# Causal attention and feed-forward block on one core: row maxima copied into the score banks by ScalarE, three score passes instead of four, and the first chunk's output projection moved into the last head pair

## The chip, the cores and the metric

One core of one Trainium2 chip runs the whole program. The metric is the device time of one execution in microseconds (us), lower is better. TensorE (PE) does matmuls, VectorE (DVE) and ScalarE (ACT) elementwise work, GpSimd (POOL) elementwise work that does not touch the matmul results, SyncE (SP) issues the DMAs.

## What is computed

From the reference, cut to what matters (two sequences of 2048 rows, model width 256, 16 heads of width 64, hidden width 768, all in fp32):

```python
hn = layernorm(h) * gamma + beta
q, k, v = rope(hn @ Wq + bq), rope(hn @ Wk + bk), hn @ Wv + bv
attn = softmax(where(tril, q @ k.T / 8, -inf)) @ v
x = layernorm(h + (attn @ Wo + bo + h))
gate, up = x @ wg, x @ wu                      # weights are int32 / 127
out = layernorm(x + (silu(gate) * up) @ wd)
```

## The kernel before

**Two stages.** The first does the attention, head pair by head pair: 8 pairs for each of 2 sequences, 16 iterations, called FIRST, MIDDLE, SWITCH (where the sequence changes) and LAST. The second is the output projection and the feed-forward, in 8 chunks of 512 rows. Matrix operands are held as a high part (`fp32r`) and a remainder, and a product is three matmuls: high by high, remainder by high, high by remainder (`product`, L1017 to L1020).

**One pair.** The scores are computed transposed, keys on partitions, in 40 units of 128 keys by up to 512 queries (`UNITS`: block of 512 queries, key tile). 28 units have all 512 queries; on the diagonal there are also four each of 384, 256 and 128. Two units make a group, 20 groups `g` make a pair. For each unit, both heads go through the array side by side (two halves of 64 rows, banks `s_ps[two]` and `s_ps[two + 1]`): three passes for the product (L1084, L1086, L1088) and a fourth (L1090) that adds minus the row's maximum, a matmul of a constant `ones_r` with `aux`. `aux` holds the negated maxima of 512 queries as rows. Diagonal units add a mask (L1094). Then ScalarE takes the exponent of both banks into `pt` (L517), TensorE multiplies by the values (`weigh`, L1115, one group later), and GpSimd adds `pt` up for the softmax sum (L458). `pt` has 5 slots, and the score banks hold two units.

**Maxima.** They are found ahead of the scores, by matmuls in the other orientation (`maxima`, L1063, bank pair `m_ps`) and a max reduction on VectorE (L731) into `mc`; the next matmul into `m_ps` waits for the reduction (`maxed`). In each group, one goes before the scores and one behind them; `AHEAD` is how many units they are ahead. For a block of 512 queries VectorE then spreads the eight columns of `mc` into the zeroed `mz` (`spread`, L745), TensorE transposes `mz` (L1101) and ScalarE copies the result to `aux` (L501).

**Work for the next pair.** Within a pair the next pair's projections are made through one shared bank `x_ps`. The table `XUSE` says which group uses that bank for what: Q0 to Q3 and K0 to K3 are the pieces of the query and key projection, V0 to V3 the values, M the transpose of maxima, R the softmax sums (`sums`, L1122). A Q or K piece goes: six matmuls; ScalarE adds the bias (`piece_raw`, L490); four DMAs swap halves; VectorE multiplies by the cosine (L764), one group later by the sine (L770) and adds (L774); another group later ScalarE rounds (`piece_hi`, L495) and VectorE forms the remainder (`piece_lo`, L779).

**Queues.** Every engine has its own in-order queue, written out by hand in the function `pair` of that engine. On ScalarE a group is: eviction of an output block, `piece_hi`, two exponents, `weights`, `shifts` (the copy to `aux`), `piece_raw`. On VectorE: spread, turn of the sums, cosine, values, the reductions, sine and add, division of an output block, `piece_lo`.

**Second stage.** For each chunk: `load_o` brings the attention output back from memory, `attn_hi` on ScalarE (L525) and `attn_lo` on VectorE (L803) split it into `o_t`, `project_out` multiplies by `Wo` (96 matmuls into `y_ps`), `add_residual` and `first_norm` make `x1_g`, `turn_x1` transposes it, `ffn_up` is 72 matmuls into `gu_ps`, `hidden` is the work of ScalarE and VectorE on them, `ffn_down` is 72 matmuls into `z_ps`, `second_norm` ends the chunk. `cycle(c)` on TensorE is `ffn_up(c)`, `turn_x1(c + 1)`, `project_out(c + 2)`, `ffn_down(c)`. The splits of chunk c + 2 are done one in each step of `hidden(c)`, the last ones behind it.

## Time and profile before

| | |
|---|---|
| median of 3 runs | 2352.92 us (2342.64 to 2354.73) |
| profiled execution | 2344.87 us, its span 2343.1 us |
| mean granted TensorE clock | 0.964 |
| busy, share of the span | PE 92%, PE weight loads 60%, DVE 72%, ACT 41%, POOL 61% |
| attention stage | to about 1970 us of the span |
| output projection and feed-forward | from there to 2343 us |
| one MIDDLE pair | about 116 us |
| DMA | 100.45 MB, mean 43 GB/s |

Matmuls are pipelined, so a matmul's duration is longer than the time until the next one may start; starts of successive rows tell the pace. The two heads' matmuls of one pass run side by side and stand in one row as x2.

### The profile page before, as it was taken

The page shows a single profiled execution, that of the slowest core. Times are in us where ns is not written, and L with a number is a line of the kernel's source. Part 1 is how long each engine was busy: PE and PEld are TensorE (multiplying, and loading weights), DVE is VectorE, ACT ScalarE, POOL GpSimd, SP SyncE. Part 2 cuts the span into 40 slices and gives each one's busy share as a digit, 9 for nine tenths or more (in the row PEclk, how much of TensorE's full clock was granted, in tenths as well). Part 3 has the DMA queues.
Part 4 walks back from the last instruction along what each step waited for, and adds up shares of the span by engine and source line. Part 5 has one row for each costly group of instructions (what it writes and reads, how often), then busy time and mean ns, then how long its engine had stood idle before and what let it go on. Part 6 is the DMA issues. An engine that isn't in the chain of part 4 may idle for free.

```text
span 2343.1 us, 43529 instructions
## 1 busy us (share of the span) xinstructions
PE 2155.6 (92%) x15872; PEld 1415.6 (60%) x15872; DVE 1685.4 (72%) x2313; ACT 957.0 (41%) x1300; POOL 1433.4 (61%) x1204
## 2 busy tenths in 40 slices
PE   5689999999999999899999999999999996898997
PEld 4446565556555655555656565656565654787886
DVE  8567878787878787778787878787878762556544
ACT  3333444344444443334444444343434443334332
POOL 2447777777777777577878787777777785000000
PEclk8799999999999999899999999999999998899998
DMA  5100111011101112101010101010101031212200
GB/s 162 62 19 24 40 31 34 28 38 30 34 27 39 32 33 67 28 24 40 24 40 24 40 24 41 24 41 24 40 24 41 23 109 54 90 64 70 91 9 28
DMA packets 79468, 100.45 MB, mean 43 GB/s; under 512 B 13968, under 2 KB 43664, under 8 KB 78992
## 3 DMA queue, kind: packets, MB, share of 16 engines
q1 hardware_dynamic: 79248, 97.60, 14.0%
q8 instruction: 128, 2.10, 0.4%
q14 instruction: 92, 0.75, 0.1%
HBM read 40.93 MB, written 23.07 MB: 27 GB/s over the span
## 4 chain that ended last, share of the span: by engine, by line
PE 74%; DVE 17%; issue 5%; ACT 1%; DMA 1%; SPq 1%; POOL 0%; DVEq 0%; POOLq 0%; ACTq 0%
PE o_ps L1115 17%; PE m_ps L1063 8%; DVE mpart L731 6%; PE x_ps L1018 6%; PE s_ps L1084 5%; PE x_ps L1020 4%; PE x_ps L1019 4%; PE s_ps L1086 4%; PE s_ps L1090 4%; PE s_ps L1088 4%; PE gu_ps L1018 2%; PE gu_ps L1020 2%; PE gu_ps L1019 2%; PE y_ps L1018 2%; PE x_ps L1122 2%
## 5 line engine op out<-in xcount | busy, mean ns | idle before, releaser
L458 POOL TENSOR_TENSOR acc<-acc,pt 128x512 f32<-128x512 f32 (+3 forms) x1024 | 1233.8, 1236 | 227.0 <-ACT pt L517 226.3
L731 DVE TENSOR_REDUCE mpart<-m_ps 128x2 f32<-128x1024 f32 (+2 forms) x576 | 625.7, 1086 | 346.7 <-PE m_ps L1063 209.7
L517 ACT ACTIVATE pt<-s_ps 128x1024 f32<-128x1024 f32 (+3 forms) x640 | 545.1, 896 | 568.3 <-PE s_ps L1090 319.0
L1115 PE MATMUL o_ps<-pt,v 128*64 128x512 f32 (+3 forms) x2560 | 558.5, 558 | 1.5 <-ACT pt L517 1.5
L1063 PE MATMUL m_ps<-qk 64*128 64x512 f32 (+3 forms) x1280 | 286.1, 442 | 97.2 <-DVE mpart L731 79.4
L1063 PEld LDWEIGHTS m_ps<-qk 64*128 64x128 f32 x1280 | 122.0, 186 | 378.0 <-issue 217.0
L1115 PEld LDWEIGHTS o_ps<-pt,v 128*64 128x64 f32 x2560 | 159.3, 139 | 236.7 <-issue 213.6
L453 POOL TENSOR_TENSOR acc<-pt 128x512 f32<-128x512 f32 (+1 forms) x128 | 165.1, 1310 | 204.1 <-ACT pt L517 204.1
L1084 PE MATMUL s_ps<-qk 64*128 64x512 f32 (+3 forms) x1280 | 249.2, 384 | 0.0
L1086 PE MATMUL s_ps<-qk 64*128 64x512 f32 (+3 forms) x1280 | 235.6, 363 | 0.0
L1090 PE MATMUL s_ps<-aux,ones_r 64*128 64x512 f32 (+3 forms) x1280 | 235.6, 362 | 0.0
L1088 PE MATMUL s_ps<-qk 64*128 64x512 f32 (+3 forms) x1280 | 234.9, 361 | 0.0
L495 ACT ACTIVATE qk<-qc 128x512 fp32r<-128x512 f32 x128 | 80.4, 631 | 289.3 <-DVE qc L774 289.3
L774 DVE TENSOR_TENSOR qc<-qc,rot 128x512 f32<-128x512 f32 x128 | 174.3, 1362 | 4.4
L1018 PE MATMUL x_ps<-w_hl,hn 128*128 128x128 f32 x496 | 140.6, 284 | 0.0
L1020 PE MATMUL x_ps<-w_hl,hn 128*128 128x128 f32 x496 | 137.7, 278 | 0.0
L1019 PE MATMUL x_ps<-w_hl,hn 128*128 128x128 f32 x496 | 137.6, 278 | 0.0
L490 ACT ACTIVATE qr<-x_ps,b_qk 128x512 f32<-128x512 f32 x120 | 82.4, 687 | 132.3 <-PE x_ps L1020 132.3
L770 DVE TENSOR_TENSOR rot<-rot,sin_sb 128x512 f32<-128x512 f32 x128 | 128.1, 1001 | 8.0 <-DMA rot<-qr 8.0
L1086 PEld LDWEIGHTS s_ps<-qk 64*128 64x128 f32 x1280 | 122.4, 186 | 18.7
L1088 PEld LDWEIGHTS s_ps<-qk 64*128 64x128 f32 x1280 | 122.0, 185 | 19.3
L1090 PEld LDWEIGHTS s_ps<-aux,ones_r 64*128 64x128 f32 x1280 | 122.1, 186 | 19.1
(151 smaller groups left out, 3426.0 us busy)
## 6 DMA issues: line engine op xcount, KB each, us to landing
rot<-qr SPq DMA_DIRECT2D x512, 64.0 KB, 2.0
attn<-o_n SPq DMA_DIRECT2D x64, 256.0 KB, 2.1
o_raw<-attn SPq DMA_DIRECT2D x8, 2048.0 KB, 8.9
w_raw<-in_wqkv SPq DMA_DIRECT2D x51, 128.0 KB, 2.6
h_g<-in_h SPq DMA_DIRECT2D x8, 512.0 KB, 3.5
out<-out_g SPq DMA_DIRECT2D x8, 512.0 KB, 3.2
qk_place<-in_h SPq DMA_DIRECT2D x4, 512.0 KB, 5.5
pt<-in_h SPq DMA_DIRECT2D x4, 512.0 KB, 11.0
```

What stands on the lines that cost most here:

```text
L458: nc.gpsimd.tensor_tensor(sums, sums, probs, ALU.add).then_inc(summed, 1)
L517: nc.scalar.activation(pt[:, u % SLOTS, :, q0:NB], s_ps[:, two:two + 2, q0:NB], ACT.Exp, scale=SCALE)\
L731: nc.vector.tensor_reduce(dst, m_ps[:, :, 0:w], AX.X, ALU.max, negate=True).then_inc(maxed, 1)
L1018: nc.tensor.matmul(dst, lhs[0], rhs[0], start=first, stop=False)
L1019: nc.tensor.matmul(dst, lhs[1], rhs[0], start=False, stop=False)
L1020: return nc.tensor.matmul(dst, lhs[0], rhs[1], start=False, stop=last)
L1063: last = nc.tensor.matmul(m_ps[:, a, 0:w], qk[par][rows, 0, q], qk[par][rows, 1, k], start=True, stop=not diag)
L1084: nc.tensor.matmul(dst[a], qk[par][rows, 1, k], qk[par][rows, 0, q], start=True, stop=False)
L1086: nc.tensor.matmul(dst[a], qk[par][rows, 1, k], qk[par][rows, 2, q], start=False, stop=False)
L1088: nc.tensor.matmul(dst[a], qk[par][rows, 3, k], qk[par][rows, 0, q], start=False, stop=False)
L1090: last = nc.tensor.matmul(dst[a], ones_r[rows, :], aux[rows, q0:NB], start=False, stop=not diag)
L1115: last = nc.tensor.matmul(o_ps[rows, q0:NB], v[par][:, j, rows], pt[:, u % SLOTS, a, q0:NB], start=(j == 0), stop=(j == n - 1), skip_group ...
```

## The change

- **Score banks.** The fourth score pass is taken out, with `ones_r` and `aux`. In its place ScalarE copies the negated maxima (`shift`, both heads, 512 queries) from SBUF into the unit's two score banks before the scores (`shift_unit`, one copy of up to 128x1024 for each unit, behind the two exponents of the group before), and the three matmul passes all add onto what the bank holds (`start=False`). The scores wait for that copy (`shifted`) instead of for the exponent (`exped`). Before the first pair two identity matmuls write the two banks of the second unit once (`banks_whole`), and two copies are made ahead.
- **Transposes of maxima.** `spread` and `mz` are gone. `turn_maxima` runs once for each head: four matmuls with a column of `mc`, repeated over 128 columns, as the weights, and `id_r`, the identity as `fp32r`, as the data, so that all 128 partitions get the row. ScalarE evicts each of the two into `shift`. The second head's turn follows behind `weigh` of the same group, and waits for ScalarE's eviction of the first.
- **Order.** `AHEAD` is 20 instead of 18; `XUSE` is rearranged; VectorE does cosine and values before it turns the sums.
- **Start.** VectorE makes `id_r` before its first statistics, so it waits for `ln_in`, the third of three small loads that follow the input on the DMA queue.
- **Last pair.** The feed-forward weights are split in groups 5, 7, 9, 11 instead of 9, 11, 13, 15. In groups 12 to 19 the first chunk's attention output is split into buffers of its own (`o_first`), and its projection runs before the last `weigh` and the last `sums`; its residual and norm run before the last division.
- **Second stage.** Chunk 0's `ffn_up` comes before chunk 1's projection. The splits of the chunk ahead start `EARLY = 4` steps before `hidden` and so end earlier. The last chunk's final norm and store are done in two halves.

The core of the diff (buffers, semaphores and wait values left out):

```diff
-AHEAD = 18
+AHEAD = 20
-XUSE = {0: "R3", 1: "M1", 2: "R0", 3: "Q0", 4: "K0", 5: "M2", 6: "R1", 7: "Q1", 8: "K1", 9: "V0", 10: "Q2", 11: "M3",
-        12: "R2", 13: "K2", 14: "V1", 15: "Q3", 16: "V2", 17: "K3", 18: "V3", 19: "M0"}
+XUSE = {3: "Q0", 4: "M20", 5: "K0", 6: "V0", 7: "Q1", 8: "K1", 9: "Q2", 10: "M30", 11: "K2", 12: "V1", 13: "Q3",
+        14: "V2", 15: "K3", 16: "V3", 17: "M01", 19: "M11"}
+SUMMED = {0: 3, 2: 0, 6: 1, 12: 2}
-FFN_SPLIT = {9: 0, 11: 1, 13: 2, 15: 3}
+FFN_SPLIT = {5: 0, 7: 1, 9: 2, 11: 3}
+OUT_SPLIT = {g: range(g - 12, g - 11) for g in range(12, 20)}
...
+            def shift_unit(n, u, first=False):
+                blk, j, q0 = UNITS[u]
+                two = 2 * (u % 2)
+                if not first:
+                    act.wait_ge(exped, n * NU + (u - 1))
+                if j <= 1:
+                    act.wait_ge(shift_in, n * (2 * BLOCKS) + 2 * (blk + 1))
+                nc.scalar.activation(s_ps[:, two:two + 2, q0:NB], shift[:, blk % 2, :, q0:NB], ACT.Copy)\
+                  .then_inc(shifted, 1)
...
                     for u in group_units(g):
                         exp_unit(kind, it, u)
+                    for u in group_units(g + 1):
+                        if not first_shift and (u < NU or kind is not LAST):
+                            shift_unit(it + u // NU, u % NU)
...
+            dve.wait_ge(ln_in, 16 * 3)
+            nc.vector.tensor_copy(id_r[:, :], id_f[:, :]).then_inc(id_rounded, 1)
             input_group(0)
...
             def scores(kind, it, par, u):
-                if kind is not FIRST or u >= 2:
-                    pe.wait_ge(exped, it * NU + (u - 1))
+                pe.wait_ge(shifted, it * NU + (u + 1))
...
                 for a, rows in enumerate(halves):
-                    nc.tensor.matmul(dst[a], qk[par][rows, 1, k], qk[par][rows, 0, q], start=True, stop=False)
+                    nc.tensor.matmul(dst[a], qk[par][rows, 1, k], qk[par][rows, 0, q], start=False, stop=False,
+                                     skip_group_check=True)
...
-                for a, rows in enumerate(halves):
-                    last = nc.tensor.matmul(dst[a], ones_r[rows, :], aux[rows, q0:NB], start=False, stop=not diag)
...
-            def turn_maxima(n, blk):
-                pe.wait_ge(mz_done, n * BLOCKS + (blk + 1))
+            def turn_maxima(n, blk, a):
...
                 for t in range(TG):
-                    last = nc.tensor.transpose(x_ps[:, t * P:(t + 1) * P], mz[:, t, :], id_f[:, :])
+                    last = nc.tensor.matmul(x_ps[:, t * P:(t + 1) * P], mc[:, blk, t, a:a + 1].broadcast_to([P, P]),
+                                            id_r[:, :], start=True, stop=True)
...
             def hidden(c, ahead):
+                if ahead is not None:
+                    for k in range(EARLY):
+                        attn_hi(ahead, k)
...
-            pe.wait_ge(cw_lo, 4)
             pe.wait_ge(maxed, 2 * PAIRS * NM)
             pe.wait_ge(c_lo, OC)
-            project_out(0)
+            project_out(0, o_first)
+            weigh(LAST, FINAL, 1, NG - 1)
+            pe.wait_ge(r_turned, FINAL * BLOCKS + 3)
+            sums(FINAL, BLOCKS - 1)
+            turn_x1(0)
+            ffn_up(0, True)
             pe.wait_ge(c_lo, 2 * OC)
             pe.wait_ge(x_added, 1)
             project_out(1)
-            turn_x1(0)
-            ffn_up(0, True)
+            ffn_down(0)
+            next_turn(0)
             next_out(0)
-            next_turn(0)
-            ffn_down(0)
```

## Rows read from the trace of the kernel before

**Rows 1.** Stretches, one MIDDLE and the LAST: PE, PEld, DVE, ACT, POOL; clock; DMA.

```profile
1256.00:1372.00 116.00, 112.89 (x866) 68.63 (x866) 91.09 (x110) 49.99 (x65) 88.90 (x75) 0.99 0.12 32
...
1838.00:1970.00 132.00, 118.10 (x894) 65.50 (x890) 69.07 (x79) 57.48 (x69) 110.17 (x96) 0.95 0.16 55
```

**Rows 2.** Timeline of VectorE, one group with pieces in work (in brackets: idle before).

```profile
1454.66 0.74 DVE L764 SCALAR_TENSOR_TENSOR qc<-x_ps,b_qk,cos_sb 128x512 f32<-128x512 f32 x1
1455.32 1.21 DVE L731 TENSOR_REDUCE mpart<-m_ps 128x2 f32<-128x1024 f32 x1
1457.18 1.23 DVE L731 TENSOR_REDUCE mpart<-m_ps 128x2 f32<-128x1024 f32 x1 [0.65 <-PE m_ps L1063]
...
1459.08 1.65 DVE L774 TENSOR_TENSOR qc<-qc,rot 128x512 f32<-128x512 f32 x1
1460.65 1.76 DVE L779 TENSOR_TENSOR qk<-qc,qk 128x512 fp32r<-128x512 f32 x1
```

**Rows 3.** Timeline at the end of the last pair.

```profile
1932.90 34.46 POOL L458 TENSOR_TENSOR acc<-acc,pt 128x512 f32<-128x512 f32 x28 [0.25 <-ACT pt L517]
...
1967.50 1.97 PE L1122 MATMUL x_ps<-acc,ones_f 128*64 128x512 f32 x4 [8.14 <-POOL acc L458]
1976.95 0.55 PE L1018 MATMUL y_ps<-wo_hl,o_t 128*128 128x256 f32 x1 [7.47 <-DVE o_t L803]
```

**Rows 4.** Waits from 2050 us on (total us, times, longest).

```profile
PE y_ps L1018 <- DVE o_t L803: 18.1, 5, 3.6
```

**Rows 5.** Timeline of TensorE, end of one unit (start, duration).

```profile
1456.29 0.39 PE L1088 MATMUL s_ps<-qk 64*128 64x512 f32 x2
1456.52 0.40 PE L1090 MATMUL s_ps<-aux,ones_r 64*128 64x512 f32 x2
```

**Rows 6.** Timeline of TensorE, the transposes of maxima and what follows.

```profile
1402.60 0.66 PE L1101 MATMUL x_ps<-id_f,mz 128*128 128x128 f32 x4
1403.18 1.72 PE L1115 MATMUL o_ps<-pt,v 128*64 128x512 f32 x8
```

**Rows 7.** Groups by line and shape (count, busy us, mean ns, idle before).

```profile
L517 ACT ACTIVATE pt<-s_ps 128x1024 f32<-128x1024 f32 x448 | 440.3, 1025 | 482.5 <-PE s_ps L1090 319.0 <-PE s_ps L1094 161.4 <-POOL acc L458 2.0
...
L745 DVE COPY mz<-mc 128x8 f32<-128x8 f32 x64 | 51.0, 797 | 0.1
...
L627 ACT ACTIVATE x_keep<-x_g 128x1024 f32<-128x1024 f32 x8 | 8.5, 1058 | 14.8 <-DVE out_g L979 14.8
```

**Rows 8.** Timeline of ScalarE in the same groups.

```profile
1452.80 0.69 ACT L490 ACTIVATE qr<-x_ps,b_qk 128x512 f32<-128x512 f32 x1 [0.81 <-PE x_ps L1020]
1454.77 0.63 ACT L495 ACTIVATE qk<-qc 128x512 fp32r<-128x512 f32 x1 [1.29 <-DVE qc L774]
1456.04 1.95 ACT L517 ACTIVATE pt<-s_ps 128x1024 f32<-128x1024 f32 x2 [0.63 <-PE s_ps L1090]
```

**Rows 9.** Timeline at the start of the span: DVE's statistics, PE's first transpose.

```profile
4.48 1.40 DVE L690 BATCH_NORM_STATS2 stats<-qk_place 128x6 f32<-128x256 f32 x4 [2.78 <-DMA qk_place<-in_h]
...
10.22 1.11 PE L1032 MATMUL s_ps<-id_f,qk_place 128*128 128x128 f32 x4 [10.22 <-DMA bet<-in_beta]
```

**Rows 10.** Groups by line: add in the pairs, remainder in the second stage.

```profile
L774 DVE TENSOR_TENSOR qc<-qc,rot 128x512 f32<-128x512 f32 x128 | 174.3, 1362 | 4.4
...
L803 DVE TENSOR_TENSOR o_t<-o_raw,o_t 128x512 fp32r<-128x512 f32 x64 | 42.1, 683 | 0.0
```

**Rows 11.** Busy time by stretch: first projection, first ffn_up, first ffn_down.

```profile
1976.90:1990.40 13.50, 13.33 (x96) 13.15 (x96) 0.01 (x1) 0.03 (x1) 0.00 (x0) 0.87 0.45 158
...
2012.60:2029.00 16.40, 16.32 (x72) 13.44 (x72) 9.93 (x16) 9.10 (x16) 0.00 (x0) 1.00 0.10 32
...
2048.70:2057.30 8.60, 8.60 (x73) 8.56 (x72) 7.25 (x19) 2.92 (x5) 0.00 (x0) 1.00 0.21 64
```

**Rows 12.** Timeline at the end of the span: VectorE's last chunk, SyncE's store.

```profile
2334.35 1.23 DVE L979 SCALAR_TENSOR_TENSOR out_g<-z_ps,x_keep 128x1024 f32<-128x1024 f32 x1 [6.48 <-PE z_ps L1020]
...
2339.65 0.37 SPq L323 DMA_DIRECT2D out<-out_g  x1
```

More of the change, by code:

```diff
@@ L82, in sem @@
             return ctx.enter_context(nc.semaphore(name))
+        with nc.sbuf_tensor("o_first_hi", [P, OC * NB], F32R) as o_first_hi:
+            pass
         cos_sb = sb("cos_sb", [P, SEQ], F32)
@@ L152, in postln_block_kernel @@
         wo_hl = split_sb("wo_hl", OC * DM)
+        with nc.sbuf_tensor("o_first_lo", [P, OC * NB], F32R) as o_first_lo:
+            pass
+        o_first = [o_first_hi[:, :], o_first_lo[:, :]]
         wg_raw = sb("wg_raw", [P, KC * HID], I32)[:, :]
@@ L555, in pair @@
                         split_ffn(FFN_SPLIT[g])
+                    if g in OUT_SPLIT and kind is LAST:
+                        for k in OUT_SPLIT[g]:
+                            act.wait_ge(cw_lo, 4)
+                            attn_hi(0, k, o_first)
             def affine(i):
@@ L609, in _ @@
             rounded(3)
-            shifts(0, 0)
+            for a in range(2):
+                shifts(0, 0, a)
             for i in range(TURNS):
                 next_affine(i)
+            act.wait_ge(cos_done, 8)
+            act.wait_ge(banks_whole, 1)
+            for u in range(2):
+                shift_unit(0, u, True)
             each_pair(act, pair)
@@ L840, in pair @@
                         split_ffn(FFN_SPLIT[g])
+                    if g in OUT_SPLIT and kind is LAST:
+                        for k in OUT_SPLIT[g]:
+                            attn_lo(0, k, o_first)
             def rest(i):
@@ L898, in _ @@
             for m in range(TG):
[L899 removed]
+                maximum(0, m, False)
             turned(2)
             remainders(1)
[L902 removed]
             unturned(3)
@@ L955, in hidden @@
             def hidden(c, ahead):
+                if ahead is not None:
+                    for k in range(EARLY):
+                        attn_lo(ahead, k)
                 for m in range(MC + 1):
@@ L968, in hidden @@
                           .then_inc(hid_lo, 1)
-                    if ahead and m < MC:
-                        attn_lo(c + 2, m)
-                if ahead:
-                    for k in range(MC, OC):
-                        attn_lo(c + 2, k)
+                    if ahead is not None and EARLY + m < OC:
+                        attn_lo(ahead, EARLY + m)
             def second_norm(c, par, n):
@@ L983, in second_norm, with last_norm, cycle @@
                 nc.vector.memset(pause[:, :], 0.0).then_inc(tile_done, 1)
-            def cycle(c, par, ahead):
+            def last_norm(half):
+                c, before = CHUNKS - 1, (2 * CHUNKS - 1) * (2 * TG + 1)
+                tiles = range(HALF_TILES * half, HALF_TILES * (half + 1))
+                here = slice(tiles[0] * DM, (tiles[-1] + 1) * DM)
+                dve.wait_ge(z_done, c + 1 + half)
+                if half == 0:
+                    dve.wait_ge(x_kept, c + 1)
+                    dve.wait_ge(out_stored, c * 16 + 16)
+                nc.vector.scalar_tensor_tensor(out_g[:, here], z_ps[:, here], DEQ, x1_keep[c % 2][:, here],
+                                               ALU.mult, ALU.add).then_inc(z_added, 1)
+                dve.wait_ge(z_added, c + 2 + half)
+                norm(out_g, 2 * CHUNKS - 1 + half, out_rows, before + half * (2 * HALF_TILES + 1), tiles)
+                dve.wait_ge(out_rows, c * TG + HALF_TILES * (half + 1))
+                nc.vector.memset(pause[:, :], 0.0).then_inc(tile_done, 1)
+            def cycle(c, par, ahead=None):
                 hidden(c, ahead)
@@ L988, in cycle @@
                 second_norm(c - 1, 1 - par, c * 2 + 1)
-                if ahead:
+                if ahead is not None:
                     add_residual(c + 2)
                     first_norm(c + 2, c * 2 + 2)
-            for k in range(OC):
-                attn_lo(0, k)
-            add_residual(0, True)
-            for k in range(OC):
-                attn_lo(1, k)
-            first_norm(0, 0)
-            x1_lo(0)
-            add_residual(1)
-            hidden(0, True)
-            first_norm(1, 1)
+            add_residual(0, True)
+            first_norm(0, 0)
+            turn_sums(FINAL, BLOCKS - 1)
+            invert(FINAL, BLOCKS - 1)
+            divide(FINAL, BLOCKS - 1)
+            x1_lo(0)
+            hidden(0, 1)
+            add_residual(1)
+            first_norm(1, 1)
+            for k in range(OC):
+                attn_lo(2, k)
             x1_lo(1)
@@ L1216, in _, with project_out @@
             pe.wait_ge(v_done, 4)
+            for i in range(2, 4):
+                last = nc.tensor.matmul(s_ps[:, i, :], id_r[:, :], hn[:, 0, 0, 0:NB], start=True, stop=True)
+            last.then_inc(banks_whole, 1)
             each_pair(pe, pair)
-            weigh(LAST, FINAL, 1, NG - 1)
-            pe.wait_ge(r_turned, FINAL * BLOCKS + 3)
-            sums(FINAL, BLOCKS - 1)
-            def project_out(c):
+            def project_out(c, src=o_t):
                 for t in range(TG):
```

274 lines of the change are left out of this document (144 added, 130 removed).

## The prediction

> **What bounds the kernel now.** I read the busy time by stretch first, then the timelines of one middle pair engine by engine, then the waits. A middle pair takes about 116 us, and TensorE is busy for 112.9 of them at a clock of 0.99; VectorE is busy for 91.1, GpSimd for 88.9, ScalarE for 50.0 [rows 1]. The reader is to see that TensorE sets the pace but that two engines stand only a fifth behind it, so a saving on TensorE can't be taken in full. In each group TensorE can't pass its second maxima until VectorE has reduced the first; with pieces in work VectorE needs from 1454.66 to 1462.41, 7.75 us, for one group, its wait for the second maxima included [rows 2]. The last pair is another stage: it takes 132 us, GpSimd is busy for 110.2 [rows 1] and works without a pause over the last 34.5 us [rows 3]. The second stage is TensorE again, with gaps in which it waits for the split of the attention output [rows 3, 4].
>
> **The score passes.** One pass over 512 queries costs TensorE 0.23 us, 1456.29 to 1456.52; the two heads run side by side [rows 5]. The durations in the row, 0.39, overlap and would give twice as much. The 40 units of a pair have 28 x 512 + 4 x (384 + 256 + 128) = 17,408 of 20,480 queries, 0.85, so a pair saves 40 x 0.23 x 0.85 = 7.8 us.
>
> **The transposes.** Four of them now take 0.58 us (1402.60 to 1403.18) [rows 6]; four times that is 2.3 us a pair. Eight sets replace them. I take 0.5 us each, 4.0 us: they are no wider than those. Bounds are 0.3 and 0.66. That gives back 1.7 us. A second turn also waits for ScalarE to evict the first. Where the next group is narrow (M20, M30) the eviction comes in time, since `weigh` covers it. For M01 ScalarE stands behind two exponents and two copies until about 5.2 us after the group's first score, and TensorE is there at 4.1: 1.1 us. For M11 I count 0.4. Together 1.5 us. So TensorE's own path is 7.8 - 1.7 - 1.5 = 4.6 us shorter.
>
> **The copies on ScalarE.** No copy from SBUF into a score bank is in this trace. The nearest rows are the exponent of 1024 columns, 1025 ns and 0.98 us from one to the next, and the SBUF copy of 1024, 1058 ns [rows 7, 8]. I take the exponent's pace, 34 us a pair; bounds are 0.7 and 1.5 us for a full unit. With four more evictions ScalarE goes from 50 to about 87 us of a pair, so it isn't full. Its place in the chain matters more. A group of 512s with a Q or K piece would take TensorE 6 x 0.23 for the scores, 0.66 for maxima, 1.6 for the piece and 1.9 for `weigh`: 5.5 us. In it ScalarE starts exponents 0.9 us in, ends them at 2.9, ends the two copies at 4.8, and only then evicts the piece (`piece_raw`, 0.69 [rows 8]), at 5.5 instead of 4.5. The next group's first scores can start at 3.9 as far as the copy goes. This is covered, with 1.6 us to spare; groups without a piece (3.9 us) have nothing to spare and stall 0.1 to 0.3 us, eight of them a pair. Queued behind a late `piece_raw` are the swap DMAs and the cosine, and behind the cosine the reductions.
>
> **VectorE.** It loses the spread, 0.8 us x 4 = 3.2 us a pair [rows 7], and gets the second maxima 0.23 to 0.46 us earlier. In the stretch of groups 7 to 10, whose pieces are on VectorE at the same time, it still needs 6 to 7.5 us a group where TensorE would need 5.5. I take 1.5 us a pair more waiting for maxima than now and 1.5 us for the small stalls and the late cosine, and against them the 3 us by which spreads no longer delay the reductions: nothing net. This is a choice between the bounds, not a reading. A middle pair then saves 4.6 us. Bounds: 0 (VectorE and ScalarE keep the pace that TensorE gives up) and 7.0 (the wait for the spread was in the way too and no new stall appears). 14 such pairs: 64 us.
>
> **Start and first pair.** VectorE now waits for the small loads, which are in at 10.2 us, where its statistics began at 4.48 [rows 9]. Of the 5.7 us, 2.2 are absorbed where it later waits for a weight split; 3.6 us remain. Two turns and evictions ahead of the first pair, two copies before its first scores and one before its third group: 1.2 + 1.9 + 1.9. Its own saving is small, since the first maxima bind it: 3.6 us. Net loss 5 us; bounds 0 and 9.
>
> **Last pair.** GpSimd sets it, so three passes save nothing behind group 6. Eight remainders move in beside it. The add on VectorE takes 1362 ns beside a busy GpSimd, and the same form takes 683 ns where GpSimd is idle [rows 10]: the two get in each other's way. The weight splits leave groups 12 to 15 for it. I take 0; bounds are 4 us less and 8 x 0.68 = 5.5 us more.
>
> That speaks against the change, and the Trainium skill has the rule (SBUF — State Buffer, Who interferes with whom): a VectorE instruction with two SBUF inputs and a GpSimd one that reads SBUF exclude each other for the whole instruction. By this rule each remainder put into the last pair would lengthen the engine that sets its end, and the sum would be 5.5 us higher than mine. The row agrees that there is interference and doesn't show who pays.
>
> **Second stage, first chunks.** Now TensorE idles 8.1 and 7.5 us around the last sums [rows 3], and the first projection takes 13.5 us at a clock of 0.87; the reader may compare 72 matmuls of `ffn_down` at 1.00 in 8.6, which is 11.5 us for 96 [rows 11]. With the change the projection runs while GpSimd finishes, ends at about 1973 in the old time, and residual, norm (6 us), a last division on VectorE (2.4) and the transposes bring `ffn_up(0)` to about 1983. Then 18 us for it (a cold start), 11.5 + 8.6 for projection 1 and `ffn_down(0)`, 1 + 1.4 for transposes and a wait, 11.5 for projection 2: 2035, where `ffn_up(1)` began at 2057.3. That saves 22 us; bounds 14 and 27.
>
> **Five later chunks.** Each now waits 3.6 us for the split, 18.1 in all [rows 4], after which its projection runs for 13.3 us instead of 11.5. With four splits ahead, all eight are done by the fourth step of `hidden`, some 8 us before TensorE asks. 5 x (3.6 + 1.8) = 27 us less; I take 26, bounds 12 and 29. Next late would be the x1 split, which has the whole projection as cover.
>
> **The end.** From TensorE's last result to the store issue are 5.3 us [rows 12]; of the second half about 3.3 remain, and its store is half as large: 2.5 us less.
>
> **Sum.** 5 - 64 + 0 - 22 - 26 - 2.5 = -109.5. The profiled execution took 2344.9 us for a span of 2343.1; the median is 2352.9, 8 us above it, and I take the difference off the median: 2243.4, say 2244.
>
> **Rivals.** (1) The whole pass comes through: 7 us a pair, 34 more than forecast, 2210. For it: TensorE waits for VectorE only a few us a pair; against it: VectorE's busy groups [rows 2], which a faster TensorE runs into. (2) The pairs give nothing, because VectorE and the longer chain through ScalarE hold the old pace: 14 x 4.6 back, 2308. For it speaks that VectorE's group of 7.75 us is longer than TensorE's of 5.5 [rows 2]; against it, that such groups are few and the spread leaves it. (3) On the other side: ScalarE becomes the bound. If a copy into the score banks costs 1.5 us, a full group with a piece has 1.95 + 3.0 + 0.69 + 0.63 = 6.3 us of ScalarE against 5.5, and with the fixed order each of some 14 full groups grows by 0.7 or more: 9 us a pair over the forecast, 14 x 9 = 126 more, 2370. It decides from about 1.4 us a copy, where the pairs lose as much as the second stage gives. For it: ScalarE doubles its load in the loop; against it: both nearest rows are at 1.05.
>
> **Chances.** Forecast (pairs save 2.5 to 6 us each) 0.57, its own range 2218 to 2276; rival 1 0.12; rival 2 0.23; rival 3 0.08. Leaving out rival 3 and the far edges of 1 and 2, the range is 2203 to 2314. A change within 0.5%, 12 us, is about what a measurement of this kernel can't tell from none. Faster: the first three cases but the worst tenth of rival 2, 0.89. The rest of that and the mild part of rival 3 make 0.04 for the same. Slower: 0.07.
>
> **What would show it.** The profile of the changed kernel should show three rows of L-numbers under `s_ps` with starts 0.23 apart, 640 copies of `shift` near 1.0 us, a middle pair of about 111.5 us with ScalarE at 87, VectorE at 88, `y_ps` without a wait in the later chunks, the first projection before the last `x_ps` sums, and VectorE's first statistics after 10 us. Wrong would make it: copies much over 1 us, waits of the scores for `shifted`, waits of `m_ps` for the reductions above 10 us a pair, or a last pair that GpSimd ends later by more than 5 us.

## The result and the profile after

The changed kernel takes 2482.5 us, median of 4 runs (2471.2 to 2488.0), against 2353.8 for the kernel before in the same set. The ratio is 1.0551, 95% interval 1.0504 to 1.0597: 129 us slower. The forecast was 2244. The profiled execution has a span of 2477.1 us at a mean granted clock of 0.940, where the span before was 2343.1 at 0.964.

The loss has one place. Milestones are the first score of the second pair, the first score of the last pair, the first matmul of `ffn_up(1)`, and the end:

| stretch | before, us | after, us | difference | forecast |
|---|---|---|---|---|
| start and first pair | 222.2 | 241.8 | +19.6 | +5 |
| 14 pairs | 1648.1 | 1799.9 | +151.8 | -64 |
| last pair to `ffn_up(1)` | 186.7 | 173.0 | -13.7 | -22 |
| `ffn_up(1)` to the end | 286.1 | 262.4 | -23.7 | -28.5 |
| span | 2343.1 | 2477.1 | +134.0 | -109.5 |

So the last two stretches gave 37 of the 50.5 us forecast, and the 14 pairs missed by 216 us. Within those pairs the loss sits in groups 6 to 14, where most of the pieces stand: they took 53.2 us of a pair before and take 66.1 now, the other eleven groups 64.5 and 62.5 (means of the 14 pairs, from one group's first score to the next's). The busy time of those 14 pairs, of the kernel before:

```profile
222.20:1870.30 1648.10, 1584.13 (x12100) 967.41 (x12098) 1287.06 (x1534) 702.76 (x918) 1241.85 (x1036) 0.98 0.12 33
```

and of the changed one, with one quiet pair of it below (columns as in [rows 1], whose first row it answers to):

```profile
241.80:2041.70 1799.90, 1602.31 (x11204) 935.51 (x11204) 1326.43 (x1478) 1164.78 (x1535) 1227.12 (x1036) 0.95 0.11 30
...
1406.83:1530.84 124.01, 108.97 (x806) 64.14 (x806) 94.38 (x105) 83.19 (x110) 87.86 (x74) 0.99 0.11 31
```

TensorE's idle time went from 64.0 to 197.6 us. That is 133.6 of the 151.8. The rest is busy time, which grew by 18 although a pass is gone. Part of that is the clock: a mean of 0.95 between the two levels of 1.2 and 2.4 GHz means a tenth of the stretch at the lower one, 180 us, where 0.98 meant 66. At most half of that difference, 57 us, is lost by it (an estimate; the rounding of the two means leaves 40 to 74). ScalarE, at 83 of 124 us, is not full.

The copies cost what was forecast, 1035 ns for a full one beside an exponent of 1023 (groups by shape, changed kernel; compare [rows 7]):

```profile
L531 ACT ACTIVATE s_ps<-shift 128x1024 f32<-128x1024 f32 x448 | 446.4, 1035 | 1.0 <-issue 0.9
L548 ACT ACTIVATE pt<-s_ps 128x1024 f32<-128x1024 f32 x448 | 438.1, 1023 | 383.1 <-PE s_ps L1141 312.5 <-PE s_ps L1146 68.4 <-POOL acc L478 2.1
```

What TensorE waits for (total, times, longest) in those 14 pairs, before:

```profile
PE m_ps L1063 <- DVE mpart L731: 56.4, 59, 4.0
PE m_ps L1063 <- issue: 5.9, 4, 1.8
```

and changed:

```profile
PE m_ps L1115 <- DVE mpart L780: 101.8, 90, 6.0
PE m_ps L1115 <- DVE mc L780: 33.7, 20, 2.2
PE x_ps L1180 <- DVE v L792: 27.1, 25, 1.6
PE m_ps L1115 <- issue: 11.7, 4, 3.4
PE x_ps L1158 <- ACT shift L521: 11.4, 14, 0.9
```

VectorE's share grew from 56.4 to 162.6 us, 106 of the 133.6. The same list over the whole run, before:

```profile
PE m_ps L1063 <- DVE mpart L731: 79.4, 81, 4.0
```

and changed:

```profile
PE m_ps L1115 <- DVE mpart L780: 133.1, 117, 6.0
PE m_ps L1115 <- DVE mc L780: 37.6, 25, 2.2
PE x_ps L1180 <- DVE v L792: 27.6, 27, 1.6
PE x_ps L1158 <- ACT shift L521: 18.3, 17, 5.1
PE m_ps L1115 <- issue: 11.7, 4, 3.4
```

Three of the five name VectorE. Its operations with two SBUF inputs also became longer: the add and the remainder (L774 and L779 before) and the division (L798 before) took 1362 [rows 10], 1004 and 772 ns and now, in the groups by line, take (mean ns behind the comma)

```profile
L812 DVE TENSOR_TENSOR qc<-qc,rot 128x512 f32<-128x512 f32 x128 | 193.6, 1512 | 4.4
L817 DVE TENSOR_TENSOR qk<-qc,qk 128x512 fp32r<-128x512 f32 x128 | 168.9, 1322 | 0.0
L836 DVE TENSOR_TENSOR o_n<-o_sum,r_b 128x512 f32<-128x512 f32 x64 | 65.0, 1016 | 7.0 <-DVE r_b L830 0.3
```

With the sine product (L770 before, 128.1 us; L808 now, 138.5) these four lines took 480 us of VectorE before and take 566, 86 more, where the spreads that went had taken 51 [rows 7].

The wait for `v` was not in the forecast at all. Here it is in the timeline of the quiet pair, group 6, in which a values piece and block 1's sums now share the bank:

```profile
1440.52 1.66 DVE L808 TENSOR_TENSOR rot<-rot,sin_sb 128x512 f32<-128x512 f32 x1
...
1442.10 0.87 PE L1173 MATMUL o_ps<-pt,v 128*64 128x256 f32 x8
1442.21 1.65 DVE L812 TENSOR_TENSOR qc<-qc,rot 128x512 f32<-128x512 f32 x1
...
1443.78 0.68 DVE L792 TENSOR_TENSOR v<-x_ps,b_v 128x512 f32<-128x512 f32 x1
...
1444.59 1.08 PE L1180 MATMUL x_ps<-acc,ones_f 128*64 128x512 f32 x4 [1.62 <-DVE v L792]
1445.60 0.50 PE L1115 MATMUL m_ps<-qk 64*128 64x512 f32 x2
1445.71 0.72 DVE L822 STREAM_TRANSPOSE r_t<-x_ps 128x512 f32<-128x512 f32 x1 [1.25 <-PE x_ps L1180]
...
1446.35 1.19 DVE L780 TENSOR_REDUCE mpart<-m_ps 128x2 f32<-128x1024 f32 x1
```

The last piece matmul started at 1441.89, so the values could have been taken out at about 1442.2. VectorE, in its fixed order, did the sine product and the addition first, and the sums waited 1.62 us. Then VectorE stood 1.25 us for those sums, with the next reduction queued behind. In group 10 the reduction stands behind four other jobs:

```profile
1462.48 1.54 DVE L808 TENSOR_TENSOR rot<-rot,sin_sb 128x512 f32<-128x512 f32 x1
...
1464.05 1.65 DVE L812 TENSOR_TENSOR qc<-qc,rot 128x512 f32<-128x512 f32 x1
...
1465.62 1.76 DVE L817 TENSOR_TENSOR qk<-qc,qk 128x512 fp32r<-128x512 f32 x1
...
1467.31 0.74 DVE L802 SCALAR_TENSOR_TENSOR qc<-x_ps,b_qk,cos_sb 128x512 f32<-128x512 f32 x1
...
1467.97 0.41 DVE L780 TENSOR_REDUCE mc<-m_ps 128x2 fp32r<-128x256 f32 x1
...
1468.43 0.39 PE L1115 MATMUL m_ps<-qk 64*128 64x256 f32 x2 [2.02 <-DVE mc L780]
```

The maxima were ready at about 1464.9; the reduction took 0.41 us and began 3.1 us later.

### The profile page after: what moved, and what is told of

It reads as the page before. It is cut to its first block, busy times and chain, and to the rows that moved or that the text cites. A ratio compares the mean times of both kernels' runs of the same rounds, so it can differ in the third digit from the quotient of the medians.

```text
span 2477.1 us, 42394 instructions
## 1 busy us (share of the span) xinstructions
PE 2169.4 (88%) x14850; PEld 1368.9 (55%) x14850; DVE 1730.0 (70%) x2255; ACT 1486.7 (60%) x2005; POOL 1420.2 (57%) x1204
## 4 chain that ended last, share of the span: by engine, by line
PE 46%; DVE 23%; issue 15%; ACT 6%; DMA 2%; POOL 2%; SPq 2%; DVEq 0%; ACTq 0%; POOLq 0%
PE o_ps L1173 10%; DVE mpart L780 10%; PE m_ps L1115 7%; PE x_ps L1180 3%; DVE rot L808 3%; PE x_ps L1070 2%; ACT pt L548 2%; DMA rot<-qr 2%; ACT s_ps L531 2%; POOL acc L478 2%; PE x_ps L1072 2%; PE x_ps L1071 2%; PE s_ps L1135 2%; SPq L348 2%; PE x_ps L1158 2%
## 5 line engine op out<-in xcount | busy, mean ns | idle before, releaser
L478 POOL TENSOR_TENSOR acc<-acc,pt 128x512 f32<-128x512 f32 (+3 forms) x1024 | 1216.6, 1223 | 387.7 <-ACT pt L548 387.1
L780 DVE TENSOR_REDUCE mpart<-m_ps 128x2 f32<-128x1024 f32 (+2 forms) x576 | 625.8, 1086 | 390.3 <-PE m_ps L1115 236.3
L1173 PE MATMUL o_ps<-pt,v 128*64 128x512 f32 (+3 forms) x2560 | 579.1, 576 | 0.0
L531 ACT ACTIVATE s_ps<-shift 128x1024 f32<-128x1024 f32 (+3 forms) x640 | 551.1, 906 | 1.0 <-issue 0.9
L1115 PE MATMUL m_ps<-qk 64*128 64x512 f32 (+3 forms) x1280 | 306.1, 474 | 196.2 <-DVE mpart L780 133.1
L1135 PE MATMUL s_ps<-qk 64*128 64x512 f32 (+3 forms) x1280 | 254.8, 394 | 4.4 <-ACT s_ps L531 4.4
L1141 PE MATMUL s_ps<-qk 64*128 64x512 f32 (+3 forms) x1280 | 238.5, 367 | 0.0
L1138 PE MATMUL s_ps<-qk 64*128 64x512 f32 (+3 forms) x1280 | 238.5, 368 | 0.0
L812 DVE TENSOR_TENSOR qc<-qc,rot 128x512 f32<-128x512 f32 x128 | 193.6, 1512 | 4.4
L817 DVE TENSOR_TENSOR qk<-qc,qk 128x512 fp32r<-128x512 f32 x128 | 168.9, 1322 | 0.0
L521 ACT ACTIVATE shift<-x_ps 128x512 f32<-128x512 f32 x128 | 76.6, 598 | 117.3 <-PE x_ps L1158 117.3
L808 DVE TENSOR_TENSOR rot<-rot,sin_sb 128x512 f32<-128x512 f32 x128 | 138.5, 1082 | 8.0 <-DMA rot<-qr 6.3
L1070 PE MATMUL x_ps<-w_hl,hn 128*128 128x128 f32 x496 | 142.7, 288 | 0.0
L1072 PE MATMUL x_ps<-w_hl,hn 128*128 128x128 f32 x496 | 140.6, 283 | 0.0
L1071 PE MATMUL x_ps<-w_hl,hn 128*128 128x128 f32 x496 | 139.9, 282 | 0.0
L1135 PEld LDWEIGHTS s_ps<-qk 64*128 64x128 f32 x1280 | 126.2, 193 | 24.5 <-ACT s_ps L531 15.7
L1138 PEld LDWEIGHTS s_ps<-qk 64*128 64x128 f32 x1280 | 125.3, 192 | 19.8
```

Of the source, the lines that this page charges most:

```text
L478: nc.gpsimd.tensor_tensor(sums, sums, probs, ALU.add).then_inc(summed, 1)
L531: nc.scalar.activation(s_ps[:, two:two + 2, q0:NB], shift[:, blk % 2, :, q0:NB], ACT.Copy)\
L780: nc.vector.tensor_reduce(dst, m_ps[:, :, 0:w], AX.X, ALU.max, negate=True).then_inc(maxed, 1)
L808: nc.vector.tensor_tensor(rot[:, a, :], rot[:, a, :], sin_sb[:, NB * c:NB * (c + 1)], ALU.mult)\
L812: nc.vector.tensor_tensor(qc[:, c % 2, a, :], qc[:, c % 2, a, :], rot[:, a, :], ALU.add).then_inc(roped, 1)
L1070: nc.tensor.matmul(dst, lhs[0], rhs[0], start=first, stop=False)
```

## The experiments

Each run's ratio is to the kernel before on the same chip; 1% is 23.5 us. The 95% intervals are plus or minus 0.002 to 0.005. "Against the changed kernel" is the difference of the ratios in us, so good to some 12 to 16 us. Where the text gives pairs or groups without a trace, they are times from first score to first score, as means of the 14 pairs: 117.7 us a pair before, 128.6 in the changed kernel.

| run | median us | ratio | against the changed kernel |
|---|---|---|---|
| e1 the end alone | 2312.9 | 0.9843 | |
| e13 the scores alone | 2506.6 | 1.0691 | |
| e2 sums in groups of their own | 2551.4 | 1.0852 | +71 |
| e3 no copies | 2447.1 | 1.0405 | -34 |
| e5 fourth pass again | 2481.3 | 1.0557 | +1 |
| e7 second maxima late | 2554.9 | 1.0868 | +74 |
| e6 first reduction ahead | 2461.7 | 1.0474 | -18 |
| e9 values between | 2447.7 | 1.0423 | -30 |
| e10 both | 2422.6 | 1.0330 | -52 |
| e14 and a turn off the loop's edge | 2418.0 | 1.0308 | -57 |
| e4 / e8 halved reductions, changed / before | 2356.6 / 2268.0 | 1.0030 / 0.9651 | -122 / (-82 of before) |
| e11 / e12 halved additions, changed / before | 2362.7 / 2287.9 | 1.0080 / 0.9759 | -111 / (-57 of before) |
| e15 e10 with halved reductions | 2314.9 | 0.9884 | -157 |
| e17 with halved additions too | 2214.5 | 0.9436 | -262 |
| e18 instead without copies | 2243.8 | 0.9559 | -233 |
| e16 the end, and first reduction ahead | 2293.6 | 0.9777 | |

### Which half loses (e1, e13)

e1 is the kernel before with the change's edits from the last pair on (`FFN_SPLIT`, `OUT_SPLIT`, `o_first`, `EARLY`, the new order of chunks, the last chunk in halves); e13 is the rest of the change (`AHEAD`, `XUSE`, `shift`, `id_r`, VectorE's order, three passes).

> The kernel before with everything that the change does from the last pair on (first chunk's output split and projected in the last pair, four tiles split early, last chunk in halves), and none of what it does to the scores: four passes, the maxima's passes and copies of before. Theory A (the loss is in the attention pairs, and the second part of the change is worth what the two traces show from the last pair's start, 472.8 us before against 435.4 after): about 2315 us, between 2305 and 2325. Rival (the two parts lean on each other, the gain at the end came from a pair that was late anyway): 2340 to 2360.

> The other half of the first run: what the change does to the scores, and nothing of what it does from the last pair on. If the two halves add up (2482.5 changed, 2312.9 with the end alone, 2350 before): 2515 to 2525. If the gain at the end depends on the pairs: 2485 to 2510.

The end alone gains 37 us (0.9843, interval 0.9813 to 0.9873), as A said. The scores alone lose 162 (1.0691). Together that is 125 lost against 129 measured, within the intervals. The median of e13, 2506.6, is 8 us under the range for halves that add up and lies in the other one (2485 to 2510); but the kernel before was at 2344 in that set and not at 2350, and by the ratio the halves add up.

### Does the removed pass matter (e5)

```diff
+                for a, rows in enumerate(halves):
+                    nc.tensor.matmul(dst[a], qk[par][rows, 1, k], qk[par][rows, 2, q], start=False, stop=False, ...)
                 for a, rows in enumerate(halves):
                     last = nc.tensor.matmul(dst[a], qk[par][rows, 3, k], qk[par][rows, 0, q], ...
```

> The changed kernel with the fourth pass back in each score unit, as a second go at the second pass (it adds that term twice, so the scores are not the reference's). Everything else stays, the copies too. Theory A2 (between the two maxima units of a group TensorE now has two score units of 0.70 us, 1.40 in all, where it had 1.86, and VectorE's 1.22 us reduction with a cosine or values of 0.7 in front no longer fits beneath; the pass that was removed was cover): the pass costs next to nothing, 2470 to 2500. Rival (TensorE is the bound, the pairs are longer for another reason): the pass costs its 7 us in each of 16 pairs, 2580 to 2600.

A whole pass put back, 7.8 us of TensorE in every pair by the forecast's count, costs nothing, as A2 said; the waits for `mpart` fall from 133.1 to 99.9 us. TensorE doesn't set these pairs. But with this cover restored the time doesn't fall either, so the missing pass is not what makes them 11 us longer; that must be in what came with it.

### ScalarE's copies (e3)

```diff
-                pe.wait_ge(shifted, it * NU + (u + 1))
+                if kind is not FIRST or u >= 2:
+                    pe.wait_ge(exped, it * NU + (u - 1))
...
-                    for u in group_units(g + 1):
-                        if not first_shift and (u < NU or kind is not LAST):
-                            shift_unit(it + u // NU, u % NU)
```

> The changed kernel without ScalarE's 640 copies of the shift into the score banks: the first of the three passes starts the bank, and waits for the exponents of two units before as the kernel before does. It leaves the maxima out of the scores (they are still reduced, turned and copied to SBUF). Theory A (VectorE's order of work and the shared bank make the pairs longer): 2440 to 2480, the pairs stay over 120 us. Rival B (the copies cost it): the pairs fall to the forecast 111 us or below, 2230 to 2300 in all.

34 us come back, not 200: rival B falls as the main cause and stays as a part. By the two traces 9.6 us of it are in the first pair (163.6 and 154.0) and 24.5 in the 14 pairs, 1.75 each. Half of that is group 17: 6.09 us from its first score to the next group's, 5.17 without the copies. There the second turn of maxima waits for ScalarE's eviction, which is queued behind two exponents and two copies.

### VectorE's order (e2, e7, e6, e9, e10, e14)

```diff
-XUSE = {3: "Q0", 4: "M20", 5: "K0", 6: "V0", 7: "Q1", 8: "K1", 9: "Q2", 10: "M30", 11: "K2", 12: "V1", 13: "Q3",
-        14: "V2", 15: "K3", 16: "V3", 17: "M01", 19: "M11"}
+XUSE = {2: "V0", 3: "Q0", 4: "M20", 5: "K0", 7: "Q1", 8: "K1", 9: "Q2", 10: "M30", 11: "K2", 13: "V1", 14: "Q3",
+        15: "V2", 16: "K3", 17: "M01", 18: "V3", 19: "M11"}
```

> The changed kernel with one edit: the shared bank's table. The sums of blocks 1 and 2 (groups 6 and 12) have the bank to themselves again; only block 0's sums, in the light group 2, share it with a values piece. Theory A1 (the pairs lose to the sums that wait in TensorE for VectorE's values and to VectorE that then waits for the sums, ahead of its reductions): about 3 us a pair come back, 2430 to 2450. Rival B (the copies on ScalarE cost it, by their chain exponents - copy - scores or by what they do to the other engines): nothing, 2475 to 2490. Rival C (VectorE simply has too much in a group, wherever the sums stand): at most 1 us a pair, 2465 to 2485.

```diff
                 for i, m in enumerate(list(ms)[:len(ms) - len(held)]):    # held = the second unit, not in FIRST
...
                         project_v(it + 1, VALUES[g], 2)
+                    for m in held:
+                        pe.wait_ge(maxed, it * NM + m)
+                        maxima(it, par, m) if m < NM else maxima(it + 1, 1 - par, m - NM)
```

> The changed kernel with TensorE's order changed in all pairs but the first: a group's second maxima unit stands behind the turn or the projection piece, ahead of the weighing, so that the reduction of the first has the two score units and the piece (1.4 us and some 2 to 2.6 us) as cover, and the next group's first unit only the weighing. Theory A2: 2400 to 2450. Rival C: 2470 to 2490, or slower where the weighing alone (about 0.9 us) is too short a cover for the second reduction.

Both miss their theory's range by 100 us and more, on the slow side; e2 lies outside every range, and e7 where its rival C said "or slower". In e2 the wait for values is gone from groups 6 and 12, and the waits of `m_ps` for `mpart` rise from 133.1 to 180.9 us: emptying TensorE's groups doesn't empty VectorE's, and the pieces pile up in the neighbours (group 7 from 5.9 to 10.4 us). In e7 a later reduction pushed cosine and values back, and TensorE waited 51 us for `qc` and 63 for `v`. Moving TensorE's work about is no remedy when VectorE's queue is what is late. The next three change that queue:

```diff
+                    early = ms[:1] if ended is None and kind is not FIRST else []   # e6; e10: after sums too
+                    for m in early:
+                        reduction(m)
                     if g - 1 in PIECE and kind is not LAST:
                         cosine(it + 1, *PIECE[g - 1], 1 - par, 2)
...
                   .then_inc(rope_mul, 1)
+                if between is not None:      # e9 and e10: values(...) in groups 6 and 12
+                    between()
```

> The changed kernel with VectorE's order changed in the groups after no sums, in all pairs but the first: the group's first reduction stands ahead of the cosine or the values of the piece before, not behind. Theory A2 (the second maxima unit waits for a reduction that stands behind another job): 1 to 4 us a pair, 2420 to 2465. Rival C (VectorE's total in a group sets the pace, the order doesn't matter): 2470 to 2490.

> The changed kernel with one job of VectorE moved: in the two groups of a pair where a values piece and sums share the bank (6 and 12), it takes the values out between the sine product and the addition of the same group, not behind both at the start of the next group. Theory A1 (the sums wait about 1.8 us in TensorE for the values, twice a pair, and the clock falls behind such a gap): 2 to 4 us a pair, 2420 to 2450. Rival (the wait only moves to VectorE, which has the same work to do): 2470 to 2490.

> The run before this, and with it each group's first reduction ahead of the cosine, the values and the turn of the sums, in every group of all pairs but the first (the values no longer depend on the next group, so this can be done after sums too). Theories A1 and A2 together: the 1.8 us waits and part of the waits for reductions go, 2380 to 2430. Rival C (VectorE's total in a group paces): within 10 us of the run before this.

All three come out as A1 and A2 said. In e9 groups 6 and 12 go from 8.9 and 7.5 us to 7.2 and 7.3, and the wait for `v` leaves the list. But the 52 us of e10 are not all a loss that the change brought. The kernel before, too, has its reductions behind the cosine and the values, and there the same early reduction gives 15 us (e16 against e1), about what it gives here (18, e6). What e9 mends, the values and sums in one group, came with the change: 30 us. Better order is worth 52 us, and some 30 of the 162 are shown to be the new order's.

```diff
-        14: "V2", 15: "K3", 16: "V3", 17: "M01", 19: "M11"}
+        14: "V2", 15: "K3", 16: "V3", 17: "M01", 18: "M11"}
```

> The kernel with values between and each first reduction ahead (2422.6), and with the next pair's second turned maxima moved from group 19 to group 18, so that the last group of a pair, behind which the loop over pairs turns back, has no wait for ScalarE's copy between two turns. Theory E (at the loop's edge TensorE stood 2.7 us for issue behind the second turn, where the kernel before stood 1.3, and the clock halved behind it, so that group 19 took 5.1 and 8.0 us by turns): 2 to 3 us per pair with an edge and a little in the others, 2395 to 2412. Rival (the edge costs the same wherever the turn stands): 2418 to 2426, or more, if group 18 grows by what 19 loses.

The move is worth 5 us, less than the intervals can tell; the median lies 6 us outside theory E's range, at the lower end of its rival's. Groups 18 and 19 together take 9.2 us in most pairs. In the four pairs that end at the loop's edge they took 15.0, 15.1, 11.8 and 11.8 us, and now take 13.9, 14.5, 11.0 and 11.4. At that edge the changed kernel (timeline; the matmul of L1138 takes 0.40 at the full clock) shows what followed an idle stretch:

```profile
1530.22 0.69 PE L1115 MATMUL m_ps<-qk 64*128 64x384 f32 x2 [2.71 <-issue]
...
1531.42 0.64 PE L1138 MATMUL s_ps<-qk 64*128 64x512 f32 x2
```

with the granted clock (last but two of the columns) at 0.76 and 0.56 around it:

```profile
1526.80:1531.80 5.00, 2.29 (x16) 1.79 (x16) 0.72 (x1) 0.60 (x1) 0.61 (x2) 0.76 0.04 10
1531.80:1536.80 5.00, 5.00 (x32) 2.57 (x28) 1.62 (x3) 3.88 (x6) 2.71 (x4) 0.56 0.00 0
1536.80:1541.80 5.00, 4.36 (x44) 2.57 (x44) 4.04 (x6) 2.74 (x4) 2.24 (x4) 1.00 0.01 2
```

### VectorE's pace (e4, e8, e11, e12)

```diff
-                nc.vector.tensor_reduce(dst, m_ps[:, :, 0:w], AX.X, ALU.max, negate=True).then_inc(maxed, 1)
+                nc.vector.tensor_reduce(dst, m_ps[:, :, 0:w // 2], AX.X, ALU.max, negate=True).then_inc(maxed, 1)
```

> The changed kernel with each reduction over the first half of its bank's columns only (the maxima are those of half the keys), so that a reduction of 1.22 us becomes about 0.65, some 44 us less of VectorE's 94 a pair... the passes are untouched. Theory A and C (TensorE waits for VectorE's reductions, 12 us more a pair than before): the waits m_ps <- VectorE go and the pairs fall to 110 or less, 2200 to 2300 us. Rival B (ScalarE's copies pace the scores): 2420 or more.

> The kernel before with each reduction over the first half of its bank's columns, as the changed kernel had it in the run before this: the control. Theory A2 (with four passes the reductions are all but covered): 1 to 2 us a pair, its waits m_ps <- VectorE were 3 on PE in the pair shown, so 2315 to 2340, against the 126 us that the same edit gave the changed kernel. Rival (the reductions pace both kernels alike): 2230 or less.

Less work on VectorE gives the changed kernel 122 us. That is 57 us short of the range of A and C: the pairs come down to 120.9 us, not to 110, so something else holds them too. It gives the kernel before 82, where I expected 10 to 35 and the rival 120 or more: that kernel was held by VectorE as well. Its waits of 79.4 us for `mpart` were the sign. With the same edit in both, the changed kernel is still 89 us behind (1.0030 against 0.9651).

```diff
-                            nc.gpsimd.tensor_tensor(sums, sums, probs, ALU.add).then_inc(summed, 1)
+                            part = slice(0, (NB - q0) // 2)
+                            nc.gpsimd.tensor_tensor(sums[:, part], sums[:, part], probs[:, part], ALU.add)...
```

> The changed kernel with GpSimd's additions of the softmax sums from each block's third unit on over half of their columns (the sums of the other half lack their terms). Theory D (the loss is made larger by GpSimd: VectorE's operations with two SBUF inputs took 1512, 1322 and 1016 ns beside it where the kernel before had 1362, 1004 and 772): these fall to 1.0, 0.8 and 0.7 us, VectorE has 8 us a pair less, 2370 to 2430. Rival (A1, A2: the waits are of order, not of pace): the operations fall, the time by less than 20 us.

> The control: the same edit in the kernel before. Theory D in its strict form (the contention is what the change brought): less than a third of what the edit gives the changed kernel, 2335 to 2350. Rival (the contention slows both, the changed kernel only stands nearer to VectorE's limit): 10 to 25 us, 2325 to 2340.

e11 ends 7 us below theory D's range. e12 goes as its rival said, both kernels gain, but its size is beyond both: 57 and 111 us, the changed kernel twice as much (46 and 108 of them in the 14 pairs). With this edit in both, the changed kernel is 75 us behind. Nothing on VectorE was edited, and its operations became shorter (groups by line, e11):

```profile
L814 DVE TENSOR_TENSOR qc<-qc,rot 128x512 f32<-128x512 f32 x128 | 147.6, 1153 | 4.4
L819 DVE TENSOR_TENSOR qk<-qc,qk 128x512 fp32r<-128x512 f32 x128 | 116.2, 911 | 0.0
L838 DVE TENSOR_TENSOR o_n<-o_sum,r_b 128x512 f32<-128x512 f32 x64 | 54.5, 852 | 7.0 <-DVE r_b L832 0.3
```

The reduction, which reads PSUM, did not (1088 ns here, 1086 in the changed kernel). The Trainium skill states the same (SBUF — State Buffer, Who interferes with whom): a VectorE instruction with two SBUF inputs contends with a GpSimd one that reads SBUF, and `tensor_reduce` on trn2 doesn't. e11 agrees on both. In e12 the picture is less even: the addition fell from 1362 to 954 ns, the remainder only from 1004 to 938, and the division rose from 772 to 942.

### What is left when both are mended (e15, e17, e18)

The edits are those above: e15 has e10's and e4's, e17 also e14's and e11's, e18 instead of e11's has e3's.

> The kernel with values between and each first reduction ahead, and with every reduction over the first half of its columns (maxima of half the keys). Theory A and C together (order and pace of VectorE are all that keeps the pairs from their forecast length): pairs of 111 to 115 us, 2230 to 2270 in all. Rival (something else too, the second turns or the copies, holds the pairs): 118 to 120, as with the halved reductions alone, 2300 to 2350.

> The kernel with VectorE's new order and halved reductions (2314.9), with the second turned maxima in group 18, and with GpSimd's additions over half their columns too (sums of half the columns lack terms). If what is left above the forecast pairs is VectorE's pace beside GpSimd: its operations with two SBUF inputs come down to about 0.9 us and the pairs to 110 to 112, 2210 to 2250. If it is the copies: 2290 to 2315.

> The same kernel with GpSimd's additions whole again and without ScalarE's 640 copies (the maxima are left out of the scores). If the copies hold what is left: 2210 to 2250. If it is VectorE beside GpSimd: 2280 to 2310, and the copies are worth at most the 35 us that they were in the changed kernel.

Order and halved reductions together leave pairs of 118 us: my claim that they are all was wrong, and the rival's 2300 to 2350 holds the result. (The turn in group 18 is in e17 and e18 too; it is worth 5 us.) GpSimd's half takes off 105 us more, the copies 76, each with those 5. Each run lands in the range that its own suspect was given, so both hold a part, and the parts overlap. How they do wasn't traced; that each shortens the way from one score to the next is my reading. With order, reductions and GpSimd relieved and the copies still in place, the pairs average 111.4 us, the length that was forecast. Two of the shorter ones (stretches, e17):

```profile
1235.94:1346.04 110.10, 105.89 (x808) 63.81 (x806) 67.36 (x105) 82.64 (x109) 57.32 (x74) 1.00 0.13 34
1346.04:1454.34 108.30, 105.81 (x806) 63.82 (x806) 67.04 (x105) 82.65 (x109) 56.80 (x74) 1.00 0.13 35
```

### A kernel that beats both (e16)

e16 is e1 with the first reduction ahead in groups after no sums, three lines as in e6.

> The kernel of the first run (four passes as before, the new end, 2312.9), and in its pairs each group's first reduction ahead of the cosine or values in groups after no sums. If the reductions' place pays with four passes too (its pairs wait some 9 us a pair for VectorE on both of TensorE's lines): 2290 to 2305. Rival (the fourth pass covers them as they stand): 2308 to 2318.

2293.6 us, in the range of its first case, ratio 0.9777 (0.9753 to 0.9801): 52 us under the kernel before, with four passes; 37 are the new end's and 15 the early reduction's. Its pairs (stretches):

```profile
1281.05:1396.89 115.84, 111.37 (x866) 68.27 (x864) 91.56 (x109) 49.98 (x65) 89.04 (x74) 1.00 0.12 33
1396.89:1511.15 114.26, 111.40 (x866) 68.41 (x866) 91.55 (x109) 49.87 (x65) 88.60 (x74) 1.00 0.12 33
```

## Why the prediction was wrong

- **The step that failed** is the one on VectorE: "nothing net. This is a choice between the bounds, not a reading", and with it its bounds, 0 to 7 us saved a pair. The pairs lost 10.8 us each. The bounds excluded a loss, on the ground that VectorE can at worst keep the pace that TensorE gives up. That holds only if its queue stays as it was. The change reordered that queue, and I priced the reordering at nothing: values and sums in one group (the sums wait behind sine and addition, 27.6 us in the run), the turn of the sums behind cosine and values, M20 to M11 moved. e9 measures 30 us for the first of these; for the others no run has a price. VectorE has 94 us of work in the quiet pair where 88 was forecast, and TensorE's waits for it in the 14 pairs went from 56.4 to 162.6 us. That is where the loss is. How it splits stays open: of the 162 us that the scores' half loses, 30 (e9) and 34 (e3) are shown by single edits, and the rest is not. No run has the kernel before with only the table and `AHEAD` of the change, or with only a pass less.
- **GpSimd.** I weighed the contention with VectorE for the last pair only. It works in every pair: halving GpSimd's additions gives 108 us in the 14 pairs, and 46 in those of the kernel before (e11, e12). With the change VectorE's four lines take 86 us more; why they became longer was not traced. The profile before had the longer operations in the middle pairs too ([rows 2], 1.65 and 1.76 us).
- **Reductions.** I counted the pairs as TensorE's. e8 shows that halved reductions give 82 us even before the change, 61 of them in the 14 pairs, with TensorE's work untouched. "A saving on TensorE can't be taken in full" was right and needed a price; that hardly any of it could be taken is my reading.
- **The score passes.** The saving is there in TensorE's busy time, and the changed kernel doesn't reach it. Busy TensorE per pair at full clock is 105.9 us with three passes and eight turns (e17), 111.4 with four and four (e16): 5.5 less, where 7.8 - 1.7 = 6.1 was forecast. In the changed kernel as it stands the pass is worth nothing (e5).
- **The copies.** Price right (1.04 against 1.0 us for a full one; ScalarE 83 us a pair against 87), and rival 3, ScalarE as the bound, is wrong with them. "Covered" fits the 14 pairs better than the total of 34 us says: of their 24.5 us, 13 are the wait of M01's second turn, which was in the forecast under the turns, and 11.5 the stalls elsewhere, 0.8 a pair. The 9.6 us of the first pair were not in it, and where VectorE is relieved the copies hold some 70.
- **The turns.** M01's wait is 0.8 us in the quiet pair where 1.1 was forecast; in all, TensorE waits 18.3 us for evictions. What the second turns cost beyond that was not isolated.
- **The clock.** Not in the forecast of the pairs. It halves behind gaps that the forecast didn't have: up to some 57 us, by the estimate above.
- **Start and first pair.** +19.6 us against +5, bounds 0 and 9. VectorE's statistics begin at 10.6 us (forecast: after 10), the first score comes 6.9 us later, and the first pair is 12.7 us longer instead of a little shorter; without the copies (e3) it is 3.1 longer. Not taken apart further. (The forecast's 5.7 less 2.2 is 3.5, not 3.6, which changes nothing.)
- **Last pair to `ffn_up(1)`.** -13.7 us against -22. The first projection runs before the last sums, as said, but starts 96.7 us from the pair's first score, behind a 2.27 us wait for the last remainder, 5.5 us later than I had it; the projection of chunk 2 took 13.1 us instead of 11.5.
- **Later chunks and end.** -23.7 us against -28.5. The 18.1 us of waits for the split [rows 4] are gone from the list, as forecast, and from the last residual addition to the end of the span it is 6.0 us instead of 8.8 [rows 12].

Rival 2 (the pairs give nothing) named the right mechanism and stopped at zero. None of the rivals had VectorE's queue, with its new order, as a loss; rival 3, the only one with longer pairs, put them on ScalarE.

## What to carry to other kernels

Before pricing an edit on the engine that is busiest, read its waits for another engine, or halve that engine's work: 79.4 us of TensorE waiting for reductions, at a busy share of 72% on VectorE, stood beside 82 us that half the reductions gave with TensorE's work untouched. When an edit changes the order of an in-order queue, follow each moved job to what is queued behind it and to who waits for that; a lower bound of "no gain" is only safe if no queue is reordered and no wait is added. And price a better order in both kernels: of the 52 us that it gave here, about 15 were to be had without the change. Cut a change in halves early: here one half gained 37 us, the other lost 162.

## What the runs showed of the hardware

- GpSimd's load changes VectorE's durations: with its additions halved (e11), the remainder on VectorE went from 1322 to 911 ns and the addition from 1512 to 1153, the PSUM reduction from 1086 to 1088.
- An SBUF to PSUM copy of 1024 columns on ScalarE takes 1035 ns, as long as an exponent from PSUM to SBUF (1023).
- A gap of 2.71 us on TensorE was followed by matmuls of 0.64 us instead of 0.40 and a granted clock of 0.76 and 0.56 over two slices of 5 us: 1.2 + 2.2 = 3.4 us of the full clock given up, at most, beside a gap of 2.71 (an estimate from the two slices).
